# The SSM head inputs are transposed by the DMA instead of TensorE, through 16-bit halves

## The reference, cut to what matters

```
proj = einsum('bld,pd->blp', hidden, in_proj_w)        # gate | x | B | C | dt ; 128 sequences of 32 positions
conv = causal depthwise convolution of (x, B, C), 4 taps;  xBC = silu(conv)
dt_p = softplus(dt + dt_bias);  dA = exp(dt_p * -exp(A_log))
state = state * dA_t + (dt_p * x)_t outer B_t ;  y_t = state . C_t      # 64 heads of 64, 8 groups of B and C
y = y + x * D;  y = rmsnorm per group of 512 channels;  y = y * norm_weight * silu(gate);  out = y @ out_proj_w.T
```

## Time and profile before

| | |
|---|---|
| median of 3 runs | 3331.65 us (3329.73 to 3332.64) |
| the profiled execution | 3330.75 us, its span 3329.0 us |
| TensorE busy | 3293.0 us, 99% |
| VectorE, ScalarE, GpSimd busy | 78%, 53%, 22% |
| mean granted TensorE clock | 0.997 of full speed |
| one pass in the middle | 45.7 us, 64 passes |

### The profile page before, as it was taken

The page is one execution under the profiler, slowest core; times in us unless marked ns, Lnnn a source line. Parts: engine busy times, 40 slices in busy tenths (PEclk is TensorE's granted clock), DMA queues, the critical chain, the costliest instruction groups (busy, mean ns, idle before and its releaser), DMA issues. The chain is left out here.

```text
span 3329.0 us, 86577 instructions
## 1 busy us (share of the span) xinstructions
PE 3293.0 (99%) x33306; PEld 2735.0 (82%) x33306; DVE 2609.7 (78%) x4367; ACT 1765.0 (53%) x3203; POOL 738.1 (22%) x520
## 2 busy tenths in 40 slices
PE   8999999999999999999999999999999999999999
PEld 6778788888888888888888888888888888888888
DVE  6787878888888888888888888888888878887443
ACT  5666665555555555555555555555555545554111
POOL 1122212222212222112222112222122221222333
PEclk9999999999999999999999999999999999999999
DMA  7433354334533364334443363435433542225331
GB/s 276 161 112 114 139 186 161 106 134 168 187 118 126 114 225 140 120 126 169 159 139 137 115 213 109 139 139 180 155 119 120 181 159 79 99 78 157 98 90 60
DMA packets 207793, 466.29 MB, mean 140 GB/s; under 512 B 35134, under 2 KB 80606, under 8 KB 198284
## 3 DMA queue, kind: packets, MB, share of 16 engines
q1 hardware_dynamic: 206364, 464.72, 41.2%
q0 software_dynamic: 368, 0.85, 0.1%
q10 hardware_dynamic: 1024, 0.27, 0.0%
HBM read 313.68 MB, written 152.09 MB: 140 GB/s over the span
## 5 line engine op out<-in xcount | busy, mean ns | idle before, releaser
L1155 PE MATMUL low_banks<-ht,wt 128*128 128x512 f32 x6144 | 1423.4, 390 | 9.3 <-DVE xc L1404 9.3
L1155 PEld LDWEIGHTS low_banks<-ht,wt 128*128 128x128 f32 x6144 | 1153.6, 188 | 258.6 <-DVE xc L1404 13.1
L1404 DVE SCALAR_TENSOR_TENSOR xc<-low_banks,cvw,xc 128x496 f32<-128x496 f32 (+2 forms) x1152 | 824.0, 717 | 221.1 <-ACT xc L1294 193.2
L1250 PE MATMUL bank<-wot,gy 128*128 128x512 f32 x3072 | 729.7, 393 | 1.2 <-DVE gy L1446 1.2
L1250 PEld LDWEIGHTS bank<-wot,gy 128*128 128x128 f32 x3072 | 567.2, 188 | 129.1 <-DVE wnext L1440 10.6
L1294 ACT ACTIVATE xc<-low_banks,cvb,cvw 128x512 f32<-128x512 f32 x384 | 298.6, 780 | 497.6 <-PE low_banks L1155 497.5
L1092 POOL TENSOR_TENSOR r<-rv,neg_half 128x4 f32<-128x4 f32 x64 | 98.4, 1537 | 1767.2 <-DVE rv L1494 1767.2
L1155 PE MATMUL bank<-ht,wt 128*128 128x512 f32 x1536 | 387.3, 401 | 0.0
L1155 PEld LDWEIGHTS bank<-ht,wt 128*128 128x128 f32 x1536 | 280.2, 189 | 55.8
L1073 POOL TENSOR_TENSOR segr<-adts,mask_le 128x1024 fp32r<-128x1024 f32 x128 | 243.1, 1921 | 351.8 <-DVE adts L1395 351.8
L1273 ACT ACTIVATE xc<-xc 128x512 f32<-128x512 f32 x384 | 241.1, 628 | 140.1 <-DVE xc L1404 139.4
(11 more groups left out here) (195 smaller groups left out, 3444.4 us busy)
## 6 DMA issues: line engine op xcount, KB each, us to landing
ht<-h_d SPq DMA_DIRECT2D x63, 2048.0 KB, 8.9
acc_d<-acc SPq DMA_DIRECT2D x64, 1024.0 KB, 4.3
wt_d<-wnext SPq DMA_DIRECT2D x112, 512.0 KB, 9.4
acc<-acc_d SPq DMA_DIRECT2D x56, 1024.0 KB, 7.0
wt<-wt_d SPq DMA_DIRECT2D x70, 512.0 KB, 6.6
stage<-in_L_attn_in_proj_w SPq DMA_DIRECT2D x84, 256.0 KB, 2.7
wot<-wt_d SPq DMA_DIRECT2D x28, 512.0 KB, 8.0
xb<-in_x SPq DMA_DIRECT2D x8, 1024.0 KB, 8.4
```

The source lines that it names most:

```text
L1155: ins = pe.matmul(pb[:, :], wt[:, n, l, k, :], ht[:, rr, k, :], start=(q == 0 and k == 0), stop=(q == 2 and k == KC - 1))
L1250: ins = pe.matmul(bank[OUT[t]][:, :], gy[:, c, l, t * P:(t + 1) * P], wot[:, rr, c, :], start=(c == 0 and q == 0), stop=(c == CT - 1 and q ...
L1404: ins = dve.scalar_tensor_tensor(dst, src, cvw[:, n, TAPS - 1 - k:TAPS - k], dst, ALU.mult, ALU.add)
```

## The change

The 16 transpositions on TensorE (`turn_x`), the four PSUM copies on ScalarE (`dtx`) and their buffer are gone. In their place, for each of the four x chunks c:

- `split(c)` on ScalarE copies the 512 fp32 values of each channel as 1024 16-bit halves into `xhalf[c]`, low halves first and then high halves, so that each half is a plane of its own. It lies in the second half of `gy`.
- `turn_x(it, c)` on SyncE waits for the split and issues one DMA transposition, xhalf[c] (128 partitions x 1024 halves of 16 bits, 256 KB) to `thalf[c]` (8 squares of 128x128). thalf[0] and [1] lie over `m`, thalf[2] and [3] over xhalf[0] and [1], so for c = 2 and 3 it also waits until transposition c - 2 has landed.
- `join_x(it, c)` on GpSimd waits for the landing and interleaves the halves to fp32 again, into `xturn`, from which the scan now reads.

GpSimd's order in a pass (`between`) is: join 0, join 1, the decay products, join 2, join 3. The conv chunks change places: x takes 0 to 3, B and C take 4 and 5, in weights, parameters and loops. On SyncE the four `turn_x` stand behind the load of the residual block; in the last pass of a group they stand between the weight loads 1 and 2, 2 and 3, 3 and 4, 4 and 5.

```diff
@@ weight_rows
-    first = ([2 * INNER + g * NS, 2 * INNER + GN + g * NS] + [INNER + g * GI + c * P for c in range(CT)]
+    first = ([INNER + g * GI + c * P for c in range(CT)] + [2 * INNER + g * NS, 2 * INNER + GN + g * NS]
              + [g * GI + c * P for c in range(CT)])
@@ attend_part, places
-    dtx = sb("dtx", [P, TT, GI])
+    xturn = sb("xturn", [P, CT, TT, P])
+    xhalf = nc.alloc_sbuf_tensor_at("xhalf", [P, CT, 2, BLK], U16, offset=gy_at + 8 * TT * HG * L)
+    over_m, over_half = gy_at, gy_at + 8 * TT * HG * L
+    thalf = [nc.alloc_sbuf_tensor_at(f"thalf{c}", [P, 2 * TT, P], U16, offset=(over_m, over_half)[c // 2] + 4 * BLK * (c % 2))
+             for c in range(CT)]
@@ sync_part
+        def turn_x(it, c):
+
+            sp.wait_ge(s_xsplit, CT * it + c + 1)
+            sp.sem_inc(s_xgo, 1)
+            if c >= 2:
+                sp.wait_ge(s_xdma[c - 2], 16 * it + 16)
+                sp.sem_inc(s_xgo, 1)
+            sp.dma_start_transpose(thalf[c][:, :, :], xhalf[:, c, :, :].rearrange("p a n -> p (a n)")).then_inc(s_xdma[c], 16)
@@ sync_part, step
             if not first:
                 sp.dma_start(acc[:, :, :], acc_v[j]).then_inc(s_accin, 16)
+            if not turn:
+                for c in range(CT):
+                    turn_x(it, c)
             if turn:
                 for n in range(NPJ - 1):
+                    if 2 <= n < 2 + CT:
+                        turn_x(it, n - 2)
                     sp.wait_ge(s_proj, NPJ * it + n + 1)
@@ gpsimd_part
+        def join_x(it, c):
+
+            pool.wait_ge(s_xdma[c], 16 * it + 16)
+            pool.sem_inc(s_joingo, 1)
+            pool.tensor_copy(xturn[:, c, :, :].rearrange("p t n -> p (t n)").bitcast(U16).rearrange("p (n a) -> p a n", a=2),
+                             thalf[c][:, :, :].rearrange("p (a t) n -> p a (t n)", a=2)).then_inc(s_xjoin, 1)
+
+        def between(g, j):
+
+            it = NBLK * g + j
+            join_x(it, 0)
+            join_x(it, 1)
+            decay_products(g, j)
+            join_x(it, 2)
+            join_x(it, 3)
@@ tensor_part, attend
-            pe.wait_ge(s_silu, NCV * it + 2)
+            pe.wait_ge(s_silu, NCV * it + NCV)
...
-            pe.wait_ge(s_silu, NCV * it + NCV)
             pe.wait_ge(s_exp, SEGB * it + SEGB)
-            for t in range(TT):
-                turn_x(t)
-
-            pe.wait_ge(s_dtx, TT * it + 1)
             project(NCV + CT - 2)
 
             pe.wait_ge(s_m, SEGB * it + 2 * SEGB)
-            pe.wait_ge(s_dtx, TT * it + TT)
+            pe.wait_ge(s_xjoin, CT * it + CT)
@@ scalar_part, attend
+            def split(c):
+                act.wait_ge(s_silu, NCV * it + c + 1)
+                act.activation(xhalf[:, c, :, :], xc[:, c, :].bitcast(U16).rearrange("p (n a) -> p a n", a=2),
+                               ACT.Copy).then_inc(s_xsplit, 1)
...
             for n in range(1, NCV - 2):
                 tap(n)
                 silu(n - 1)
+                split(n - 1)
...
             tap(NCV - 1)
+            split(CT - 1)
             silu(NCV - 2)
             silu(NCV - 1)
             gate(0)
             gate(1)
-            for t in range(TT):
-                act.wait_ge(s_xt, TT * it + t + 1)
-                act.activation(dtx[:, t, :], bank[XT[t]][:, :], ACT.Copy).then_inc(s_dtx, 1)
+            act.wait_ge(s_xsplit, CT * it + CT)
```

More of the change, by code:

```diff
@@ L22 @@
 U8 = mybir.dt.uint8
+U16 = mybir.dt.uint16
 ALU = mybir.AluOpType
@@ L897, in attend_part @@
     bank = sh.bank
-    XT, SEG, CB, OUT, SSQ, NEXT = (4, 5, 6, 7), (4, 5), 3, (4, 5, 6, 7), 3, (5, 6)
+    SEG, CB, OUT, SSQ, NEXT = (4, 5), 3, (4, 5, 6, 7), 3, (5, 6)
     scanned = sh.low_banks
@@ L927, in attend_part @@
     s_exp = sem("s2_exp")
-    s_xt = sem("s2_xt")
-    s_dtx = sem("s2_dtx")
+    s_xsplit = sem("s2_x_split")
+    s_xgo = sem("s2_x_turn_may_start")
+    s_xdma = [sem(f"s2_x_turned{c}") for c in range(CT)]
+    s_xjoin = sem("s2_x_joined")
+    s_joingo = sem("s2_x_halves_there")
     s_skip = sem("s2_x_times_d")
@@ L961, in load_conv_params @@
     def load_conv_params(g, queue):
-        for lo, n, c0 in ((0, 1, INNER + g * NS), (1, 1, INNER + GN + g * NS), (2, CT, g * GI)):
+        for lo, n, c0 in ((CT, 1, INNER + g * NS), (CT + 1, 1, INNER + GN + g * NS), (0, CT, g * GI)):
             queue.dma_start(cvw[:, lo:lo + n, :], cw[ds(c0, n * P), :].rearrange("(c p) k -> p c k", p=P)).then_inc(s_cvp, 16)
@@ L1104, in gpsimd_part @@
         pool.wait_ge(sh.s_mask, 4)
-        decay_products(0, 0)
+        between(0, 0)
         root(0)
@@ L1109, in gpsimd_part @@
             scan_products(0, 1 + s)
-            pool.wait_ge(s_segr, 2 * s + 6)
-            pool.wait_ge(s_step, s + 2)
+            between(0, 1 + s)
+            pool.wait_ge(s_stepped, SEGB * s + 2 * SEGB)
+            pool.wait_ge(s_xjoin, CT * s + 2 * CT)
             rows = slice(s * L, (s + 1) * L)
@@ L1128, in scan_pass @@
             scan_products(g, j)
-            decay_products(g, j)
+            between(g, j)
             root(NBLK * g + j)
@@ L1139, in gpsimd_part @@
         scan_products(G - 1, NBLK - 1)
-        decay_products(G - 1, NBLK - 1)
+        between(G - 1, NBLK - 1)
         pool.wait_ge(s_proj, NPJ * (NIT - 1) + 7)
@@ L1157, in project @@
                 ins.then_inc(s_proj, 1)
[L1159 to L1163, removed]
             def scan(c):
@@ L1172, in scan @@
                             ins = pe.matmul(scanned[u * HP:(u + 1) * HP, b, (c * TT + t) * L:(c * TT + t + 1) * L],
-                                            dtx[rows, t, h * HP:(h + 1) * HP], m[rows, t, h, :], start=True, stop=True)
+                                            xturn[rows, c, t, u * HP:(u + 1) * HP], m[rows, t, h, :], start=True, stop=True)
                 return ins
@@ L1207, in attend @@
                     cols = slice(t * P + b * L, t * P + (b + 1) * L)
-                    ins = pe.matmul(bank[CB][b * L:(b + 1) * L, t * L:(t + 1) * L], xc[:, 0, cols], xc[:, 1, cols],
+                    ins = pe.matmul(bank[CB][b * L:(b + 1) * L, t * L:(t + 1) * L], xc[:, CT, cols], xc[:, CT + 1, cols],
                                     start=True, stop=True)
             ins.then_inc(s_cb, 1)
-            pe.wait_ge(s_silu, NCV * it + NCV)
             pe.wait_ge(s_exp, SEGB * it + SEGB)
-            for t in range(TT):
-                turn_x(t)
-            pe.wait_ge(s_dtx, TT * it + 1)
             project(NCV + CT - 2)
             pe.wait_ge(s_m, SEGB * it + 2 * SEGB)
-            pe.wait_ge(s_dtx, TT * it + TT)
+            pe.wait_ge(s_xjoin, CT * it + CT)
             pe.wait_ge(s_z, CT * it + CT + 2)
@@ L1279, in skip @@
             def skip(c):
-                act.activation(xc[:, 2 + c, :], xc[:, 2 + c, :], ACT.Copy, scale=dsk[:, c:c + 1]).then_inc(s_skip, 1)
+                act.activation(xc[:, c, :], xc[:, c, :], ACT.Copy, scale=dsk[:, c:c + 1]).then_inc(s_skip, 1)
             def high(c):
@@ L1455, in add_skip @@
                 dve.wait_ge(s_skip, CT * it + c + 1)
-                dve.tensor_tensor(by_residue(y[:, c, :]), by_residue(xc[:, 2 + c, :]),
+                dve.tensor_tensor(by_residue(y[:, c, :]), by_residue(xc[:, c, :]),
                                   scanned[:, :, c * P:(c + 1) * P].rearrange("p b (t l) -> p b t l", l=L),
```

1 line of the change is left out of this document (removed).

## The result

The median before is 3330.69 us (3328.96 to 3332.64, four runs), after it is 3494.14 us (3489.98 to 3499.3, four runs): 1.0491 times as long, 95% interval 1.0473 to 1.051. The change costs 163 us. The forecast was 3316 us and the range ended at 3420.

A forecast was written before the change was run, and what follows sets the result against it. TensorE, busy 99%, was taken as the bound, VectorE close behind. Usual passes -56, seven of the last group -12, last passes -2 and first passes +55 gave -15: 3330.75 to 3316 us, range 3280 to 3420.

The forecast's parts named there:

- The mechanism of the gain: TensorE, each of 64 passes: without the transpositions of x the scan can start 1.72 us sooner, 110 us in all.
- the 0.4 us taken off for VectorE: Output product, 56 of 64 passes: m 0.35 us later, so 0.4 us of the gain comes back as a longer wait.
- The 0.19 us: Output product in the kernel before: TensorE was read as losing this once to VectorE, called the second bound.
- The prices of the new work: Split on ScalarE 1.05 us, join on GpSimd 1.3 us, transposition landing 3.3 us after issue on an idle queue.
- Moved by 1.05 it starts m at 1018.2: VectorE ahead of the scan: the third split pushes its work by 1.05 us, so m starts 0.35 us later.
- the sum of the usual pass: 43 passes neither first nor last of a group: scan ready 1019.5, TensorE there 1020.56; gain 1.3 us each, -56.
- the DMA in a crowd: DMA engines: one transposition was taken to occupy them 1.2 us, between ends of 0.7 and 1.85 us.
- The last passes of a group: Seven passes with transpositions among weight loads: fourth chunk joined at 839.1, scan due 837.76; gain 0.3 us each, -2.
- The first passes: Seven passes, transpositions queued on SyncE behind the stored residual: scan waits 9.6 us for GpSimd, net loss 7.9 each, +55.
- Rival 2: Slower by a slow transposition, paid four times before the last chunk; at 4 us each over 3680 us; chance 0.18.
- The sign of the failure in the profile: Idle time ahead of every scan: joins over 1.6 us, transpositions over 1.7, or SyncE itself held long by issuing.
- Two in five had been put on slower: Chance of a slower kernel, 0.40: slow joins on GpSimd (0.22, 3381 us) plus slow transpositions (0.18).

The follow-up runs named there:

- e9: The changed kernel with the load of the residual block issued behind the four transpositions, except in last passes of a group: 3335.23 us, 0.9998 times before.
- e7: The changed kernel with SyncE's transpositions moved ahead of the residual load and the wot loads put behind them in the next pass: 3256.89 us, 0.9763 times before.
- e1: The kernel before, with four unused 16-bit copies of a join's size on GpSimd beside VectorE's decode, no DMA added: 3436.01 us.
- e3: The changed kernel with the four joins on ScalarE instead of GpSimd: 3397.13 us, 1.0192 times before.
- e8: The kernel before, with two unused 16-bit copies of a join's size on GpSimd in each pass: 3329.51 us.
- e2: The changed kernel with joins of 64 elements instead of 1024 in all passes but the very first: 3323.98 us.

## Why the prediction was wrong

**The mechanism of the gain was right.** Without a wait a pass is 1.65 us shorter in group 7 (forecast 1.72) and 1.63 in the usual passes of e9 and e7 (forecast 1.3; the 0.4 us taken off for VectorE did not appear: in e9 m starts 23.6 us into the pass, 0.1 later than before and not 0.35). The 0.19 us that the forecast has TensorE lose in the output product were read wrongly: they stand in the row of the weight loads, and TensorE itself has no idle time there.

**The prices of the new work held.** ScalarE: split 1.05 us, measured 1.054. GpSimd: join 1.3 us, measured 1.37 alone (the mean is 1.44 with those stretched by VectorE). Landing on an idle queue: 3.3, measured 3.0 at best. The Trainium skill's page "GPSIMD Engine Reference", 3.1, gives 1.03 cycles for each element of such a body, at 1.2 GHz an estimated 0.88 us for 1024, and no figure for what each instruction costs on top. The 1.37 us measured lie half a microsecond above that, so the value from the rows was nearer.

**The step that failed** is the sentence "Moved by 1.05 it starts m at 1018.2", with the sum of the usual pass that rests on it ("hidden, with 1.1 us to spare. Gain 1.72 - 0.4 = 1.3 us"). It counts the conv order's shift and gives VectorE's decode its old length. The decay products were placed at 1014.1 to 1016.6 and join 2 behind them to 1017.9: in the stretch in which the decode runs (1015.9 to 1018.2 by the forecast). I wrote both schedules and did not lay them over each other. In the changed kernel the decode ahead of m takes 6.3 us, m starts 1058.60 - 1030.93 = 27.67 us into the pass, where the forecast has it at 23.8. That the decode is stretched by GpSimd is shown by e1 (stretch without DMA), e3 (no stretch without joins on GpSimd) and e9 (no stretch in the usual passes when the joins come earlier).

The Trainium skill has the rule that I missed: "GPSIMD Engine Reference", 8, Key points, says that GpSimd shares its SBUF interfaces with VectorE, and contends with VectorE instructions that read two SBUF inputs or run in a faster mode with two ports. The runs agree, though the trace doesn't name the mode of an instruction, and they give the size here: a decode instruction of 0.5 us lasts until the GpSimd instruction beside it is over, some 1.5 us.

**A term mis-sized: the DMA in a crowd.** One transposition was to hold the engines 1.2 us (ends 0.7 and 1.85). Alone it does nearly that. In e9, the window in which only the third one moves (128 GB/s over 2 us are its 256 KB):

```profile
1012.00:1014.00 2.00, 2.00 (x11) 1.65 (x10) 0.30 (x1) 1.98 (x4) 2.00 (x3) 1.00 0.67 128
```

0.67 of 2 us is 1.34. Over the whole kernel it is read from the page's queue line (packets, MB, share of 16 engines), before and after:

```profile
q1 hardware_dynamic: 206364, 464.72, 41.2%
```

```profile
q1 hardware_dynamic: 476700, 531.86, 51.7%
```

(0.517 x 3488.2 - 0.412 x 3329.0) / 256 = 1.69 us; the same for e9 (51.6% of 3334.4) is 1.36. So beside other transfers one costs more: between 1044 and 1054 of the pass above the windows sum to 9.4 us of share, of which the rest of the residual load is an estimated 1.9 at 362 GB/s, so 1.9 for each. SyncE takes 1.23 us to issue one, where I had 0.4, and in a full queue up to 6.4; in the pass above the four hold it 10.4 of the 12.07 us from first to last. The residual load ahead of them lands 8.9 us after its issue, where I had 7.0. So in the usual pass x0 is there 18.8 us after the pass began, where I had 17.1, and the decay products end at 24.5 instead of 22.2: joins 2 and 3 meet the decode too. By itself that costs little. With the old lengths of decay products and joins the last join would end at about 1057.6, where TensorE is free at 1057.2: 0.4 us. But it decides how much is stretched. At the forecast's times one decay product and join 2 would lie beside the decode, as many instructions as in e8, whose passes lost nothing; 1.7 us later it is both products and both joins. So the loss of the usual pass takes both, the contention and the lateness; e2 and e3 take away the first, e9 the second. That the pass would have been near its old time at the forecast's times is an estimate from e8 and wasn't run.

**The last passes of a group** failed at another step. The forecast takes the landing of the fourth chunk, 0.04 us after the scan is due, and one join ("it lands at 837.8, is joined at 839.1"). In six of the seven passes that landing comes nearly so, 0.3 to 1.2 us after the scan is due. But the second chunk lands only 3.1 to 4.0 us ahead of that time, and behind it join 1, the decay products and joins 2 and 3 stand in a row on GpSimd: 3 x 1.37 + 2.54 = 6.65 us at their own lengths, an estimated wait of 2.6 to 3.5, and 3.9 to 4.6 measured, with about 1 us of stretching. GpSimd's queue was put at nothing there. With tiny joins (e2) the wait is 1.35 in the mean. The last passes are worth +22 us in all where I had -2. Rival 2's condition ("It decides from about 1.7 us, near my upper end, by the last passes of a group") was met in the number, 1.69, but the late landing that it speaks of is a small part of the wait.

**The first passes** were foreseen: a wait of 9.6 us for GpSimd, measured 9.7 to 12.3. TensorE in one:

```profile
914.63 3.75 PE L1204 MATMUL low_banks<-m,xturn 32*64 32x32 f32 x256 [10.05 <-POOL xturn L1106]
...
919.94 4.23 PE L1193 MATMUL bank<-ht,wt 128*128 128x512 f32 x12
```

Missing was what follows the wait: at the lower clock the scan takes 3.75 us (2.74 at full clock) and the projection 4.23 (3.00). Over the seven, scan start to the end of that projection takes 9.1 us in the mean against 6.54 at full clock. So the loss was 11 us each, +77, where I had +55.

**The account.** Forecast -15 us, measured +160 in the span. Of the 175 between: usual and second passes 37 x (2.08 + 1.3) = 125, first passes 22, last ones 24; groups 0 and 7 together were forecast right within a few us. Of the 125, e9 takes back 121 (30 x 3.71 + 7 x 1.34). Against passes without a wait (44.07) the usual and second ones lose 37 x (2.08 + 1.63) = 137 us. Of these the traces give 78 to waits ahead of the scan (2.22 us in the mean of the usual passes, 1.65 of the second ones) and 36 to the slower matmuls behind them (scan start to the end of the next projection: 7.65 us against 6.54 in the usual ones, 6.82 against 6.42 in the second ones); 9 more are waits in the output product. The clock's part is thus about a quarter.

**The sign of the failure in the profile** was half right. "An idle time ahead of every scan" came in groups 1 to 6. Two of its three reasons were there in number (a transposition over 1.7 us in a crowd, and SyncE held for long), and they make GpSimd's work late; but in the usual passes the wait is released by m on VectorE, which none of the three names. Two in five had been put on slower, for rivals that were not this one.

## What to carry to other kernels

Before work is moved to GpSimd, lay its new instructions in time over VectorE's, not only each engine over TensorE: every VectorE instruction of the contending kind is priced at the whole of the GpSimd instruction beside it, and the gap on VectorE says how much of that is free (here some 2 us). When a DMA joins a critical path, look first at what is issued ahead of it on the same queue: here a load that nobody waits for until the end of the pass cost 159 us by standing in front, behind two weight chunks; in group 7, without those chunks, the same order cost nothing.

## What the runs showed of the hardware that was not expected

- VectorE's tensor_scalar on 512 int32 or uint8 values from SBUF to SBUF (0.54 and 0.48 us alone) is stretched to the end of the GpSimd instruction beside it, copy or product, up to 1.6 us. GpSimd loses too, less: a join 1.51 for 1.37, two decay products 3.00 for 2.54. Three conv instructions with a PSUM operand keep their 2.23 us beside a join, and m and a join in e9 (both at 1020.68) leave each other alone.
- A DMA transposition of 256 KB of 16-bit halves inside SBUF moves in about 1056 packets (270340 more for 256 of them), holds the engines 1.34 us alone and 1.9 in a crowd, and lands 3.0 us after its issue at best, 10.2 at most. SyncE is held 1.23 us by each, and up to 6.4 in a full queue. The Trainium skill's page "VectorE: DVE Perf Modes", "The three transpose paths", gives 1309 ns for a 128x128 square, which would make an estimated 10.5 us of eight squares one by one: they do not add up so.
- A wait of 2.9 us ahead of the scan is followed by about 3.4 us at a granted clock of 0.50; waits of 0.55 us in every pass of e1 left the clock at 0.997.
